# Moving the last two batches' gathers and sums of a sorted expert layer into the next layer's stage

## Time and profile before

| | us |
|---|---|
| runs of the kernel before | 2011.31, 1990.44, 1989.12 |
| their median | 1990.44 |
| the profiled execution | 2005.44 |
| its span, first to last instruction | 2003.6 |
| layer2's last copy starts | 334.71 |
| layers_3_and_4 begins (first ACT instruction) | 368.99 |
| its last instruction starts | 428.88 |

### The profile page before, as it was taken

How to read it: one execution, slowest core, us unless ns; L and a number is a source line. 1 busy time by engine, 2 the same in 40 slices (tenths; PEclk the granted TensorE clock), 3 DMA queues, 4 the chain that set the end, 5 groups by cost and what they waited for, 6 DMA issues and landing times. The chain is left out here.

```text
span 2003.6 us, 50819 instructions
## 1 busy us (share of the span) xinstructions
PE 1762.4 (88%) x20087; PEld 1273.5 (64%) x20106; DVE 1241.1 (62%) x2436; ACT 1056.8 (53%) x2386; POOL 834.9 (42%) x1089
## 2 busy tenths in 40 slices
PE   7783996665799999999998779999999999999886
PEld 4332996234468888888887537888788756633332
DVE  4534444369557778787764337888878768634434
ACT  4651442457676666666654345555555541066552
POOL 1004131215357767667662005666666610044201
PEclk9996998786899999999998899999999989599998
DMA  7002784000130000000000405444444300000100
GB/s 280 1 1 84 224 259 119 9 0 1 43 138 15 24 14 24 14 14 24 14 24 25 190 2 141 130 131 135 124 128 127 106 1 1 1 2 1 38 1 22
DMA packets 51182, 131.88 MB, mean 66 GB/s; under 512 B 11288, under 2 KB 23200, under 8 KB 50048
## 3 DMA queue, kind: packets, MB, share of 16 engines
q1 hardware_dynamic: 47040, 121.24, 19.1%
q0 software_dynamic: 2816, 7.21, 1.1%
q10 hardware_dynamic: 1088, 0.13, 0.0%
HBM read 110.47 MB, written 18.09 MB: 64 GB/s over the span
## 5 line engine op out<-in xcount | busy, mean ns | idle before, releaser
L2534 DVE SCALAR_TENSOR_TENSOR big<-bank,pack,big 128x256 f32<-128x256 f32 (+2 forms) x384 | 183.0, 478 | 39.4 <-ACT mask L2423 23.9
L1982 DVE TENSOR_TENSOR hl<-bank,hh 128x512 fp32r<-128x512 f32 x192 | 132.8, 692 | 65.0 <-ACT hh L1916 55.6
L1916 ACT ACTIVATE hh<-bank 128x512 fp32r<-128x512 f32 x192 | 115.0, 599 | 83.9 <-DVE bank L1977 82.4
L2422 ACT ACTIVATE big<-bank,pack 128x256 f32<-128x256 f32 x192 | 91.3, 476 | 127.3 <-PE bank L2230 122.9
L773 PE MATMUL bank<-yh,wl 128*128 128x512 f32 x384 | 151.8, 395 | 4.9 <-DVE yl L1926 2.6
L774 PE MATMUL bank<-yl,wh 128*128 128x512 f32 x384 | 150.9, 393 | 0.0
L775 PE MATMUL bank<-yh,wh 128*128 128x512 f32 x384 | 150.6, 392 | 0.0
L1977 DVE TENSOR_TENSOR bank<-bank,a 128x512 f32<-128x512 f32 x192 | 133.2, 694 | 7.3 <-PE bank L775 1.0
L1816 POOL TENSOR_TENSOR a<-a,rep 128x512 f32<-128x512 f32 x96 | 125.3, 1306 | 29.7 <-DMA rep<-routing 25.1
L2934 ACT ACTIVATE pt<-bank 128x1024 f32<-128x1024 f32 (+3 forms) x128 | 79.5, 706 | 103.5 <-PE bank L2786 103.4
L2140 POOL TENSOR_TENSOR big<-big,mask 128x256 f32<-128x256 f32 (+1 forms) x128 | 93.7, 732 | 89.8 <-DVE big L2534 57.4
(11 more groups left out here) (600 smaller groups left out, 4500.0 us busy)
## 6 DMA issues: line engine op xcount, KB each, us to landing
rep<-routing SPq DMA_DIRECT2D x64, 384.0 KB, 3.5
big<-in_experts SPq DMA_DIRECT2D x46, 516.0 KB, 4.1
rep<-routing SPq DMA_DIRECT2D x64, 256.0 KB, 3.9
big<-in_big SPq DMA_DIRECT2D x1, 9216.0 KB, 26.3
gate<-big SPq DMA_DIRECT2D x32, 256.0 KB, 2.1
z<-gate SPq DMA_DIRECT2D x16, 512.0 KB, 3.6
rep<-routing SPq DMA_DIRECT2D x64, 128.0 KB, 3.5
pack<-in_pack SPq DMA_DIRECT2D x1, 5846.5 KB, 20.7
```

Of the source, the lines that this page charges most:

```text
L1916: nc.scalar.activation(hh[:, sl((n - 1) % 3)], up_bank(n - 1), ACT.Copy).then_inc(s["high"], 1)
L1982: nc.vector.tensor_tensor(hl[:, sl(n % 3)], up_bank(n), hh[:, sl(n % 3)].bitcast(F32), ALU.subtract).then_inc(s["low"], 1)
L2534: ins = nc.vector.scalar_tensor_tensor(out=d, in0=conv_in(i, back), scalar=weight(i, 3 - back), in1=d, op0=ALU.mult, op1=ALU.add)
```

## The change

The twelve semaphores, and the six buffers that outlive the stage (`where`, `share`, `b2`, `w8t`, `out`, `o`), are taken by a new function around both stages. `collect`, `join`, `mix` and `add` are defined once in layer2 and called from both. Group 0's batches are handled as before. layer2 ends after its last copy; the gathers of batches 2 and 3 are the whole POOL list of the next stage, and their mix, join and add stand between the steps of batches 0 and 1 there. The waits for the bias load and the flattened weights are made once, at tile 20. POOL's adds of y to x are gone; in their place `project_out` starts with a product of the identity with y.

```diff
-def layer2(nc, k, x, y, a):
+def layer2(nc, k, x, y, a, mem_after, late):
...
+        def collect(pool, b):
+            g = [b in group for group in EXPERT_GROUPS].index(True)
+            for slot in range(4):
+                pool.wait_ge(late.s[f"stored_{slot}"], 16 * len(range(slot, firsts[g + 1], 4)))
+            for t in range(TB * b, TB * b + TB):
+                for i in range(2):
+                    nc.gpsimd.indirect_dma_start(out=found(t, i), ...).then_inc(late.s[f"got_{b}"], 16)
+
+        def join(pe, b):
+            pe.wait_ge(late.s["mixed"], b + 1)
+            after(pe, late.s["done"], b)
+            nc.tensor.matmul(k.ps[7], b2[0:G, :], w8t[0:G, sl(b)], start=True, stop=False)
...
+        def mix(dve, b):
+            dve.wait_ge(late.s[f"got_{b}"], 16 * 2 * TB)
+            after(dve, late.s["joined"], b - 1)
...
+        def add(dve, b):
+            dve.wait_ge(late.s["joined"], b + 1)
+            nc.vector.tensor_tensor(x[:, sl(b)], x[:, sl(b)], k.ps[7], ALU.add).then_inc(late.s["done"], 1)
...
+            for b in range(B):
+                if b not in last:
+                    collect(pool, b)
...
+                if n == 20:
+                    pe.wait_ge(s["bias_in"], 16)
+                    pe.wait_ge(s["flat"], B)
...
-            for b in last:
-                join(b)
...
-            for i, b in enumerate(last):
-                mix(b)
-                if i:
-                    add(last[i - 1])
-            add(last[-1])
-            dve.wait_ge(s["done"], B)
+            dve.wait_ge(s["evicted"], N)
+
+
+def layers_2_to_4(nc, k, x, y, a):
+    late = Kit()
+    names = "stored_0 stored_1 stored_2 stored_3 got_0 got_1 got_2 got_3 scaled mixed joined done"
+    late.s = {n: nc.alloc_semaphore(f"{n}_{nc.next_id()}") for n in names.split()}
+    with ExitStack() as mem:
+        layer2(nc, k, x, y, a, mem, late)
+        layers_3_and_4(nc, k, x, y, a, late)
+    counted.extend(late.s.values())
...
         @block.gpsimd
         def _(pool):
-            for b in range(B):
-                pool.wait_ge(s["y_ready"], b + 1)
-                nc.gpsimd.tensor_tensor(x[:, sl(b)], x[:, sl(b)], y[:, sl(b)], ALU.add).then_inc(s["mixed"], 1)
+            for b in late.batches:
+                late.collect(pool, b)
...
                 after(pe, s["summed"], b)
-                nc.tensor.matmul(out_bank, k.w["L1_attn_w_o"], h[b % 2][:, :], start=True, stop=True).then_inc(s["proj"], 1)
+                nc.tensor.matmul(out_bank, k.ident, y[:, sl(b)], start=True, stop=False)
+                nc.tensor.matmul(out_bank, k.w["L1_attn_w_o"], h[b % 2][:, :], start=False, stop=True).then_inc(s["proj"], 1)
...
+            def late_rows(b):
+                pe.wait_ge(s["kcopied"], 1)
+                late.join(pe, b)
+                pe.wait_ge(late.s["done"], b + 1)
...
             project_in(0)
+            project_in(1)
+            project_out(0)
+            late_rows(2)
             centre(2)
-            project_in(1)
+            project_out(1)
+            late_rows(3)
             centre(3)
             variance(2)
-            project_out(0)
             variance(3)
-            project_out(1)
             project_in(2)
...
                 dve.wait_ge(s["proj"], b + 1)
-                dve.wait_ge(s["mixed"], b + 1)
...
             scan(0)
+            late.mix(dve, 2)
             scan(1)
+            late.add(dve, 2)
+            late.mix(dve, 3)
             add(0)
+            late.add(dve, 3)
             normed(2)
```

More of the change, by code:

```diff
@@ L795, in layer2 @@
     names = ("bias_in counted numbered folded cg_ready zeroed centred squared summed rooted rs_ready logits chosen placed mapped addressed normed exps shifted weighed "
-             "positions turned laid gate up silu hidden down evicted flipped flat mixed joined done chain "
-             "w_0 w_1 w_2 w_3 scattered_0 scattered_1 x_0 x_1 x_2 stored_0 stored_1 stored_2 stored_3 got_0 got_1 got_2 got_3")
+             "positions turned laid gate up silu hidden down evicted flipped flat chain "
+             "w_0 w_1 w_2 w_3 scattered_0 scattered_1 x_0 x_1 x_2")
     rows_in, rows_out = k.sorted_rows, [nc.dram_tensor(f"results_{nc.next_id()}", (n * P, D), F32).ap() for n in limits]
+    where, share, b2, w8t, out, o = (mem_after.enter_context(nc.sbuf_tensor(f"{n}_{nc.next_id()}", [P, w_], dt)) for n, w_, dt in (("where", 2 * NT, I32), ("share", 2 * NT, F32), ("b2", P, F32), ("w8t", T, F32), ("out", 4 * P, F32), ("o", 2 * S, F32)))
     with ExitStack() as mem, stage(nc, names) as (block, s):
         sb = lambda n, w_, dt=F32: mem.enter_context(nc.sbuf_tensor(f"{n}_{nc.next_id()}", [P, w_], dt))
-        cg, sq, var, b2, w8t = sb("cg", G), sb("sq", 2 * S), sb("var", NT), sb("b2", P), sb("w8t", T)
+        s = {**s, **late.s}
+        cg, sq, var = sb("cg", G), sb("sq", 2 * S), sb("var", NT)
         lg, d, rank, w8, mx, tot = (sb(n, c) for n, c in (("lg", NT * G), ("d", NT * G), ("rank", NT * G), ("w8", NT * G), ("mx", NT), ("tot", NT)))
@@ L818, in layer2 @@
         mine = lambda m, g, w_=G: m[:, blocks[g][0] * w_:(blocks[g][-1] + 1) * w_]
+        def collect(pool, b):
[4 more added lines that the diff above has]
+                for i in range(2):
+                    nc.gpsimd.indirect_dma_start(out=found(t, i), out_offset=None, in_=rows_out[g], in_offset=bass.IndirectOffsetOnAxis(where[:, i * NT + t:][:, 0:1], 0)).then_inc(late.s[f"got_{b}"], 16)
+        def join(pe, b):
+            pe.wait_ge(late.s["mixed"], b + 1)
+            after(pe, late.s["done"], b)
+            nc.tensor.matmul(k.ps[7], b2[0:G, :], w8t[0:G, sl(b)], start=True, stop=False)
+            for i in range(TB):
+                mm = nc.tensor.matmul(k.ps[7][:, sl(i, P)], o[:, b % 2 * S + i * P:][:, 0:P], k.ident, start=False, stop=i == TB - 1)
+            mm.then_inc(late.s["joined"], 1)
+        def mix(dve, b):
+            dve.wait_ge(late.s[f"got_{b}"], 16 * 2 * TB)
+            after(dve, late.s["joined"], b - 1)
+            for i in range(TB):
+                t = TB * b + i
+                cur = o[:, b % 2 * S + i * P:][:, 0:P]
+                nc.vector.tensor_scalar(cur, found(t, 0), share[:, t:t + 1], None, ALU.mult).then_inc(late.s["scaled"], 1)
+                dve.wait_ge(late.s["scaled"], t + 1)
+                mixed = nc.vector.scalar_tensor_tensor(out=cur, in0=found(t, 1), scalar=share[:, NT + t:][:, 0:1], in1=cur, op0=ALU.mult, op1=ALU.add)
+            mixed.then_inc(late.s["mixed"], 1)
+        def add(dve, b):
+            dve.wait_ge(late.s["joined"], b + 1)
+            nc.vector.tensor_tensor(x[:, sl(b)], x[:, sl(b)], k.ps[7], ALU.add).then_inc(late.s["done"], 1)
+        late.collect, late.join, late.mix, late.add, late.batches = collect, join, mix, add, last
         @block.sync
@@ L941, in flip @@
                 mm.then_inc(s["flipped"], 1)
[L943 to L951, removed]
             columns = []
@@ L1121, in evict @@
                 nc.vector.tensor_copy(out[:, sl(n % 4, P)], down_bank(n)).then_inc(s["evicted"], 1)
[L1123 to L1135, removed]
             for g, group in enumerate(EXPERT_GROUPS):
```

24 lines of the change are left out of this document (9 added, 15 removed).

## The result

The changed kernel takes 1987.65 us, the median of 20 runs (1971.48 to 1997.22). The kernel before took 1992.85, the median of 20 runs beside them. The measured ratio is 0.9945 with a 95% interval of 0.9922 to 0.9968, which is 11 us less, between 6 and 16. It is not the quotient of the medians: these lie 5.2 us apart, and the means of the same runs 8.2, so the gain may be nearer the small end of that interval. All ratios here leave out two executions at a granted clock of 0.80, one of after_again2 (2161.61 us) and one of best (2174.26).

A forecast was written before the change was run, and what follows sets the result against it. POOL's gathers were taken to bound the 34 us seam, and a PE, ACT and DVE dependence chain the scan stage. -31.85 + 9.9 + 1.7 = -20.2 us took 1990.4 to 1970.2 us, range 1964 to 1983.

The forecast's parts named there:

- The stage starts earlier: Seam after the sorted layer: the scan stage starts at 337.15 instead of 369.0, saving 31.85 us.
- rival D: Seam: the stage's end waits longer than thought, at most 2.5 us, giving 1973 us; chance 0.06.
- the 339 named as a sign of being wrong: Scan stage's start: after 339 would show the forecast wrong; near 337.2 would show it right.
- The clock at the start: Scan stage's start: PE enters at half clock as before, rising some 4.3 us in; otherwise only about 0.8 us gained.
- The gathers: Scan stage, POOL: the same sixteen gathers run from 337.83 at the old pace; dropping POOL's adds gives nothing.
- Rival C: Gathers strongly slowed: at 2.8 us each they cost 24.7 us more, giving 1994 us; chance 0.02.
- B: Gathers mildly slowed, to the scatters' worst pace: +3.6 us, giving 1974 us; chance 0.06.
- The work put into the scan stage: Middle of the scan stage: batches 2 and 3's moved work delays batch 2's variance on PE by 9.9 us.
- rival A: Middle of the scan stage: the clock falls in PE's pause, about +4 us, giving 1974 us; chance 0.14.
- x + y on PE: End of the scan stage: added identity products for batches 2 and 3 lie on the path, +1.7 us.
- The difference is local, so I carry it over: Whole kernel: the local saving of 20.2 us carries over in microseconds to the runs' median of 1990.44.
- a later layer that gives the 20 us back: Layers after the scan stage: a sign of being wrong; 0.06 was left for what changes elsewhere.

The follow-up runs named there:

- after_again2: A further unchanged copy of the changed kernel, run as reference beside three others: 2019.52 us, ratio 0.9937 to the kernel before.
- best: Changed kernel plus all four local edits and 499 already met waits in TensorE's program: 2044.00 us, ratio 1.0043 to the kernel before.
- all four local edits: Against the changed kernel: GpSimd adds y for batches 2 and 3; batch 0's sum, variance(2) and batch 2's inversion come earlier. Alone: 1974.25 us, ratio 0.9857.
- before_pe15: Kernel before plus 31 already met waits, 15 more TensorE instructions, in the sorted layer: 2036.13 us, ratio 1.0031 to the kernel before.
- after_pe0: Changed kernel with TensorE's program at before's length, by leaving out repeated waits and adding 12 met ones: 1984.15 us, ratio 0.9926 to the kernel before.
- best_pe0: Changed kernel plus all four local edits, TensorE's program at before's length (repeated waits out, 28 met waits in): 1970.86 us, ratio 0.9866 to the kernel before.
- before_again: The kernel before, run again unchanged on chip B: 2022.06 us, ratio 0.9966 to the kernel before.
- after_pe241: Changed kernel plus 483 already met waits (241 instructions), TensorE's program exactly 256 longer than before's: 2049.18 us, ratio 1.0097 to the kernel before.

## Why the prediction was wrong

By its steps, on the profiled executions of chip A:

*The stage starts earlier* (-31.85): right; 34.28 became 2.40, -31.88, against the 2.44 that the step implies. The clear did split in two at this seam (0.45 and 0.26 us for one of 0.72), at no cost, and rival D did not occur. That the stage starts at 339.33, after the 339 named as a sign of being wrong, comes from further up: the last copy is already 2.2 us later in this execution.

*The clock at the start* (half clock, as before): wrong in this trace. The clock stayed up, and the first normalisations came 2 us sooner. In seven of the eleven traces that have this seam it did fall within 1.5 us of the stage's start, so this step forecast as certain what goes either way. As that step says, batch 3's rows were then waited for (1.56 us), and most of the gain was lost again.

*The gathers*: right. 340.13 to 359.05 is 18.92 / 15 = 1.26 us a step, beside normalisations, scans and the mix, against 1.257 in the earlier trace rows. Rival C did not occur, and of B there is a trace: one step of the fifteen, beside the mix, took 1.32. In the other ten traces with this seam one or two steps beside the scan and the mix took 1.33 to 1.65, at most 0.5 us over all sixteen gathers, where the three traces of the kernel before's work have none over 1.29, with a mix beside them too. The rule of the Trainium skill that was weighed (GPSIMD Engine Reference, section Key points), by which GpSimd contends with such instructions of VectorE, goes the same way as this small effect; that it is its cause was not tested.

*The work put into the scan stage* (+9.9): too small. Variance(2) is issued 372.19 - 339.33 = 32.86 us after the stage's start, instead of 21.78 before: +11.1. The excess is rival A, which I had given 0.14 and priced at 4: the clock was lost in all six traces of this order, in three at the pause before batch 1's output product, as here, in three already at the one before the centring of batch 2. Here, from the output product to the join's second part (364.70 to 369.29), 4.59 us pass, and in the first pair at full clock 2.86 (355.24 to 358.10): 1.7 lost, against 0.6 by which that product was early (25.4 us after the stage's start, not 26.0). On chips B and C, with the late sum beside it, the copies' stretch is 4.2 and 5.7 us longer than on A. The pause came from a choice that I had read in the diff and priced ("PE stands about 2 us for this"), and putting batch 0's sum first took back 4.5 us on chip B. On chip D all four local edits together were worth 5.7.

*x + y on PE* (+1.7): right. From variance(2) to the next layer it is 41.28 us against 39.29, +2.0, and taking the product away gave 2.07 back.

Local sum: -31.88 + 11.08 + 1.99 = -18.8, where -20.2 was forecast.

*The difference is local, so I carry it over*: this step failed, and it is the larger error. Layer6's stage, which has not one changed line, takes 3.7 us longer, because the change made TensorE's program 15 instructions longer ahead of it. That is shown from both sides: 15 instructions put into the kernel before bring the loss, and the changed kernel at before's length has none of it. The prediction named "a later layer that gives the 20 us back" as a sign of being wrong, but had no cause for it and 0.06 for all of that kind.

-18.8 + 3.7 = -15.1, against -11 measured with an interval from -16 to -6. The last 4 us (7 by the means, 10 by the medians) are not settled. They are no fixed loss: the same sum gives -11.3 on chip B and -9.6 on C (with the stretch of before_pe15, 95.55, for before's), and -18.7 for after_pe0 on D, where the ratios say -9, -13 and -15.

Part of it may be the clock. With h as the us at half clock in a run (twice its span times one minus its mean clock), the 20 runs of the changed kernel lie on span = 1903.8 + 0.353 h, with a correlation of -0.96 between span and clock. The change takes 33.6 us of half clock out of the stretch (37.5 to 3.9); on chip D the mean of h fell from 248 in before to 223 in after_pe0, some 8 less than that, or 3 us. But in best_pe0 the mean fell by 37 where its stretch accounts for 31, so this return of half clock elsewhere was argued and not shown. Most of the scatter lies in one later stage, layer9's (causal attention): in the 14 traces it takes from 263.0 us at 15 us of half clock to 285.7 at 78, with no order by kernel.

The test of T.L and T.G by two such lines, named in the expectation of before_again, met neither: with the slope of 0.353 the copies' lines lie 6 us apart on chip B, where T.L wanted 19 and T.G 8 to 12. It can't decide, since the change removes 20 us of half clock from the stretch there, much of it with PE idle, and the lines charge 0.353 for each.

Two sets of runs of the same program differed by 0.34%, which is 7 us; the last 4 are inside that. With the block shift undone the ratio was 0.9926 (0.9887 to 0.9965), and the forecast's own ratio, 1970.2 / 1990.44 = 0.9898, is inside that interval; it is not inside the changed kernel's.

## What to carry to other kernels

A change in one stage can cost time in another that it does not touch, if it changes the number of an engine's instructions ahead of a dense part: when the local gain is in the trace and the total lacks it, compare every later stage from one and the same instruction, and look for "issue" idle inside groups that contain no wait. Before believing a stage's whole duration, cut it at a fixed instruction, since the clock in its sparse first part moved it by up to 4 us here. And when work is put behind transfers, put what other engines wait for ahead of the work that must wait for the data: that one line was worth 4.5 us in a pair of traces on chip B.

## What had not been expected of the hardware

- TensorE's instructions come in 16 KB packets, and in dense code PE can stand while one is on its way: up to 1.4 us, at six places of layer6's stage in before_pe15. The Trainium skill (Runtime: NRT & Kernel Launch, section Instruction fetch mechanics) gives the same block, 256 instructions, and calls the cost of crossing its boundary "mostly hidden". Of the 102 such packets in the stage most are hidden in these traces too. What those that are not cost depends on the length of the program ahead: 3.7 us more at -14, 7 and 15 than at 0 and 256. That PE waits for the packet is read from its place and time; no row names it as the releaser.
- A wait that is already met is not free on TensorE. Fifteen of these instructions in an idle stretch cost nothing that shows (the sorted layer took 240.55 us with them and 240.58 without); the 240 recorded ones in after_pe241 took from 182.5 to 232.3, 0.21 us each.
- The sorted layer took some 30 us longer on chips B and C than on A, D and E, in both kernels (240.58 against 211.30 for before). PE stands there between single products, marked "issue": 32.8 us in the copy of before on B against 1.5 on A, 18.6 against 1.4 in the changed kernel. The cause was not looked for.
